# Two accumulators for the dense sums, one bank for all placings, four to five build banks, and blanks written by GpSimd

## The reference

```python
xn = _layernorm(x)                            # x: 6250 x 256, f32
h = segment_sum((xn @ W1)[src] * edge_weight[:, None], dst, 6250)
g = segment_sum((h @ W2)[src] * edge_weight[:, None], dst, 6250)   # 200000 edges, dst sorted
x = x + g + linear_attention(xn)              # 4 heads of 64: (q (LN(k)^T LN(v))) wo + bo
x = x + moe_top2(_layernorm(x))               # 16 experts, 256 -> 512 -> 256, then a layernorm
```

## Time and profile before

| | |
|---|---|
| median of 3 runs | 3532.04 us (3525.42 to 3533.8) |
| the profiled execution | 3563.73 us |
| its span | 3561.7 us |
| its mean granted TensorE clock | 0.906 of 2.4 GHz |

### The profile page before, as it was taken

One profiled execution on the slowest core, in us unless ns is written; L12 is line 12 of the kernel. 1 busy time (PEld: TensorE's weight loads), 2 busy tenths in 40 slices (PEclk: granted clock), 3 DMA queues, 4 the chain that ended last, 5 costly groups with the idle time before them and its releaser, 6 DMA issues.

```text
span 3561.7 us, 48771 instructions
## 1 busy us (share of the span) xinstructions
PE 2840.4 (80%) x14412; PEld 2015.7 (57%) x14413; DVE 1395.8 (39%) x3855; ACT 1370.9 (38%) x2993; POOL 1922.7 (54%) x2019
## 2 busy tenths in 40 slices
PE   1799999999999999788778787888877648999930
PEld 0466556566566656555555555555556647888820
DVE  8455545455554554322222222222225641111157
ACT  4687767777777773000000000000004423333322
POOL 2555555566565564466666666666643551222235
PEclk9999999999999999888888888989888868999975
DMA  6344344344444436655555555555532334444454
GB/s 217 118 154 155 115 151 156 117 160 157 145 131 155 155 120 199 197 161 161 160 158 167 161 163 158 164 156 164 162 106 84 116 123 132 139 145 133 125 156 122
DMA packets 268415, 527.04 MB, mean 148 GB/s; under 512 B 58823, under 2 KB 155086, under 8 KB 268096
## 3 DMA queue, kind: packets, MB, share of 16 engines
q0 software_dynamic: 88848, 240.99, 22.3%
q1 hardware_dynamic: 148256, 252.66, 21.7%
q10 hardware_dynamic: 31120, 31.04, 2.7%
HBM read 394.15 MB, written 131.79 MB: 148 GB/s over the span
## 4 chain that ended last, share of the span: by engine, by line
PE 54%; another core or an unknown queue 15%; issue 11%; DVE 7%; ACT 5%; DMA 4%; SPq 2%; ACTq 0%; DVEq 0%; POOL 0%; POOLq 0%
PE bank L994 23%; PE bank L982 12%; PE sums L1008 5%; PE bank L1217 4%; DMA pa<-ys_d 3%; PE bank L1205 2%; PE bank L1018 1%; PE bank L1078 1%; ACT build L795 1%; ACT build L793 1%; PE sums L965 1%; PE bank L1027 1%; PE bank L1144 1%; ACT pa L916 1%
## 5 line engine op out<-in xcount | busy, mean ns | idle before, releaser
L688 POOL DMA_INDIRECT pa<-xn_d,srcs x816 | 783.5, 960 | 537.7 <-PE sums L1008 321.5
L994 PE MATMUL bank<-t1s,pa 128*128 128x256 f32 x2450 | 643.4, 414 | 153.9 <-ACT ob L818 83.3
L688 POOL DMA_INDIRECT pa<-h_d,srcs x544 | 528.4, 971 | 307.2 <-issue 150.3
L994 PEld LDWEIGHTS bank<-t1s,pa 128*128 128x128 f32 x2450 | 497.3, 209 | 281.9 <-issue 121.5
L982 PE MATMUL bank<-build 128*128 128x343 f32 x1500 | 514.9, 484 | 138.8 <-DVE build L1376 60.9
L994 PE MATMUL bank<-t0s,pa 128*128 128x256 f32 x2450 | 558.7, 384 | 9.8 <-DVE pa L1394 8.0
L1394 DVE TENSOR_TENSOR pa<-bank,pa 128x343 f32 x750 | 378.0, 514 | 422.0 <-PE bank L982 183.7
L994 PEld LDWEIGHTS bank<-t0s,pa 128*128 128x128 f32 x2450 | 461.3, 191 | 108.6 <-issue 48.0
L982 PEld LDWEIGHTS bank<-build 128*128 128x128 f32 x1500 | 276.5, 197 | 350.0 <-issue 278.6
L795 ACT ACTIVATE build<-build,ones 128x343 f32<-128x343 f32 x750 | 436.3, 582 | 24.4
L793 ACT ACTIVATE build<-build,tabs 128x343 f32<-128x343 f32 x750 | 424.9, 567 | 41.1 <-issue 27.4
(11 more groups left out here) (257 smaller groups left out, 2716.2 us busy)
## 6 DMA issues: line engine op xcount, KB each, us to landing
slab_d<-pa SPq DMA_DIRECT2D x175, 448.0 KB
pa<-slab_d SPq DMA_DIRECT2D x175, 448.0 KB
pa<-in_w ACTq DMA_DIRECT2D x32, 512.0 KB, 3.9
pa<-in_w SPq DMA_DIRECT2D x32, 512.0 KB, 3.6
pa<-ys_d SPq DMA_DIRECT2D x109, 130.0 KB
pa<-xn_d,srcs POOLq DMA_INDIRECT x816
pa<-eo_d SPq DMA_DIRECT2D x49, 256.0 KB, 3.1
pa<-h_d,srcs POOLq DMA_INDIRECT x544
```

The source lines that it names most:

```text
L688: pool.indirect_dma_start(gath2[b * QT + j], None, table, bass.IndirectOffsetOnAxis(ap=srcs[:, n:n + 1], axis=0)).then_inc(s_g[b], 16)
L994: ins = pe.matmul(app[:, 0:D], slab3[:, s, :], table[:, s * D:(s + 1) * D], start=s == 0, stop=s == T - 1)
```

## The change

Bank 7, until now the dense placing's, becomes the second accumulator; the accumulators (banks 4 and 7) alternate by unit. Both kinds of placing share bank 6, so each waits for both kinds of add. Of the two accumulators the one that the present unit doesn't need is lent to the builds: from the start the bank whose turn isn't now the running sum's, and after the dense placing the other one too, so that a unit's first chunks have four banks and the later ones five. `wait` in `build_banks` is the number of adds of the unit that must be done before a chunk may be built. `free_for_dense` picks the place of the dense placing, in layer 0 the first chunk from 5 on, in layer 1 the first plane from 1 on, that has no step with a placing or an add of a group near it: chunk 5 in 16 units, 12 in 4, 19 in 4; plane 1 in 12 units, 2, 3 and 4 in 4 each. DVE's dense add follows at four chunks or one plane behind. GpSimd writes the blanks with a memset, in its gather queue ahead of the gathers whose ring slot is freed at that plane or just behind it; in most units that is two blanks, one step's four gathers, two blanks, four gathers, one, four, two, and then the other gathers.

```diff
-        bld, app, plg, pld = [bank[2], bank[3], bank[5]], bank[4], bank[6], bank[7]
+        app, plc = [bank[4], bank[7]], bank[6]
...
+        blanks_at = {}
+        for i in range(NU - 1):
+            for p in range(CT):
+                behind = min(s for n in range(p, CT) for s in steps_at(i, "p", n, 0))
+                blanks_at.setdefault(behind + RING, []).append((i, p))
...
+        def build_banks(i):
+            banks, last, use, wait = [2, 3, 5, (4, 7)[i % 2]], {}, [], []
+            for m in range(KB):
+                if i > 0 and m == dense_at[0][i] + 1:
+                    banks.append((7, 4)[i % 2])
+                b = min(banks, key=lambda b: last.get(b, -1))
+                use.append(b)
+                wait.append(last.get(b, -1) + 1)
+                last[b] = m
+            return use, wait
...
+            def blank_plane(i, p):
+                pool.wait_ge(s_ap, i * CT + p + 1)
+                pool.wait_ge(s_slab[p], i * 16 + 16)
+                pool.memset(plane(p), 0.0).then_inc(s_z, 1)
+
             for s in range(STEPS):
+                for i, p in blanks_at.get(s, ()):
+                    blank_plane(i, p)
                 gathers(s, 0, xn_d)
...
-                act.activation(ob[1][:], app[:, 0:D], ACT.Copy).then_inc(s_obd, 1)
+                act.activation(ob[1][:], app[i % 2][:, 0:D], ACT.Copy).then_inc(s_obd, 1)
...
-                pe.wait_ge(s_bev, c + 1)
-                pe.matmul(bld[c % BLD][:, 0:WT], lohot[c % LR], mvs[c % MR], start=True, stop=True
+                wait_from(pe, s_bev, i * KB + wait[m])
+                pe.matmul(bank[use[m]][:, 0:WT], lohot[c % LR], mvs[c % MR], start=True, stop=True
...
-                if p == 0 and d > 0:
-                    pe.wait_ge(s_obd, d)
+                if p == 0:
+                    wait_from(pe, s_obd, d - 1 if i > 0 else d)
...
                 pe.wait_ge(s_hpd, 2 * d + 2)
-                wait_from(pe, s_pad, d)
+                wait_from(pe, s_pag, placed[0])
+                wait_from(pe, s_pad, placed[1])
...
-                    if m == 2 and i > 0:
+                    if m == dense_at[0][i]:
                         place_dense(i - 1, 0)
...
-                    if p == 1 and i > 0:
+                    if p == dense_at[1][i]:
                         place_dense(i - 1, 1)
...
+                    if i > 0 and m == dense_at[0][i] + 4:
+                        place_add(1, GU + i - 1, t1s)
                     add_chunk(i, m, at)
...
+                    if i > 0 and p == dense_at[1][i] + 1:
+                        place_add(1, GU + i - 1, t0s)
                     all_gathered(steps_at(i, "p", p, 1), 1, t0s)
```

More of the change, by code:

```diff
@@ L431, in ring_of, with free_for_dense @@
             return s % size, used + s // size, size
+        def free_for_dense(i, layer, where, last, behind):
+            for at in range(last[0], last[1]):
+                so_far = STEPS * i // NU if not layer else STEPS * max(i - 1, 0) // (NU - 1)
+                near = []
+                for n in range(KB if where == "m" else CT):
+                    for s in steps_at(i, where, n, layer):
+                        if n < at:
+                            so_far = s + 1
+                        if at - behind <= n < at + behind:
+                            near.append(s % QK)
+                if (so_far - 1) % QK != 1 and 1 not in near and 2 not in near:
+                    return at
+            assert False
+        dense_at = [[None] + [free_for_dense(i, layer, "mp"[layer], ((5, 24), (1, 6))[layer], (4, 1)[layer])
+                              for i in range(1, NU)] for layer in range(2)]
+        def build_banks(i):
[8 more added lines that the diff above has]
+            return use, wait
+        build_at = [build_banks(i) for i in range(NU)]
         def chunk_at(m):
@@ L795, in moving @@
                 act.activation(a, a, ACT.Relu, bias=ones[:, 0:1], scale=-1.0).then_inc(s_mv, 1)
-            def blanks(i, p):
-                act.wait_ge(s_ap, i * CT + p + 1)
-                act.wait_ge(s_slab[p], i * 16 + 16)
-                act.activation(plane(p), zero[:].broadcast_to([P, CT * P]), ACT.Copy).then_inc(s_z, 1)
             def takes(steps, layer):
@@ L832, in _ @@
                             moving(i + 1, m)
-                        blanks(i, p)
                     takes(steps_at(i, "p", p, 0), 0)
@@ L1010, in gathered @@
                 ins.then_inc(s_hu, 1)
+            placed = [0, 0]
             def place_gathered(u, layer):
@@ L1391, in add_chunk @@
                 dve.wait_ge(s_bmm, c + 1 + CREDIT)
-                dve.wait_ge(s_bev, c + BLD - (0 if i == NU - 1 else 1))
+                wait_from(dve, s_bev, c if i == NU - 1 else c - 1)
                 part = slab3[:, :, bass.ds(at[chunk_at(m)], W)]
-                dve.tensor_tensor(part, bld[c % BLD][:, 0:WT].rearrange("p (s w) -> p s w", w=W), part, ALU.add
+                dve.tensor_tensor(part, bank[build_at[i][0][m]][:, 0:WT].rearrange("p (s w) -> p s w", w=W), part, ALU.add
                                   ).then_inc(s_bev, 1)
@@ L1494, in _ @@
                 for p in range(CT):
-                    if p == 0 and i > 0:
-                        place_add(1, GU + i - 1, t1s)
                     if (i, p) in halves_at:
```

27 lines of the change are left out of this document (14 added, 13 removed).

## The result

The changed kernel is **slower by 0.5%**: 3552.01 us (median of 6 runs, 3543.76 to 3567.85) against 3534.14 us (6 runs, 3525.42 to 3536.34), ratio 1.0052, 95% interval 1.0032 to 1.0072. Forecast were 3441 us and a range of 3370 to 3545.

The account below looks back on a forecast made before the run. PE's work was taken to bound layer 0, the loop between gathers and PE to pace layer 1. Terms -66 - 32 - 9 + 15 = -92 us took 3563.73 to 3471.7, scaled by 0.9911 to 3441 us; range 3370 to 3545.

Parts of the forecast that it names:

- Bound of layer 0: Layer 0: PE's own work bounds it, busy 1202.6 of 1282 us, so at most 79.4 us of idle PE can be had.
- Layer 1, -66: Layer 1, second accumulator: removing apply's wait for the copy was to save 66 us, bounds -10 and -150.
- the second limit: Layer 1, gather stream: GpSimd still pauses once per ring refill, 34 x 2.3 = 78 us stay, 83 of 161.5 go.
- The first limit, 75: Layer 1, apply's wait for the accumulator copy: 75 of 83.3 us go, about 8 come back at place_dense.
- Rival A: Layer 1: late PE completions only move to place_dense and ring slots; layer 1 gives -10, total 3496 us; chance 0.20.
- Layer 0, banks, -32: Layer 0, chunk builds: four and five banks remove PE's idle time before chunks, gaining 13.5 to 50.6 us, middle -32.
- the 1.45 us tail: Layer 0, later chunks of a unit: 1.45 us each instead of 0.58, read as PE and DVE waiting on each other.
- Accumulators, shared bank, later placing in layer 0, -9: Layer 0, dense placing moved from chunk 2 to 5 to 19: its wait for the copy goes, -9 us, between -6 and -14.
- Blanks on GpSimd, +15: Layer 0, unit starts: blanks in the gather queue cost +0.4 to +0.6 us a unit over 24 units, +15 us.
- The floor of layer 0, 1221 us: Layer 0, GpSimd's minimum: 979 us of gathers, 134 of blanks and 108 of ring refills, allowing up to -61 us.
- rival C: Layer 0: blanks lengthen the gather stream instead of filling pauses, GpSimd becomes the bound; slower, 3573 us; chance 0.14.
- Rival D: Layer 0, unit starts: GpSimd's memsets hold DVE through shared ports, at worst +38 us on the sum, 3478 us; chance 0.04.

## Why the prediction was wrong, point by point

**Bound of layer 0: right in name.** PE's work bounds it, and on the 3247 us chips without a gap. The 79.4 us of idle PE in the first trace were not missing banks: with three banks and half of the gathers PE is idle for 4 of 1050 us on the 3560 us chip.

**Layer 1, -66: wrong, measured -8 in the first traces and +2 on the 3560 us chip.** The step that failed is the second limit, that GpSimd would pause once in each refill, 34 times, and 83 of its 161.5 us would go. It rested on nothing but the size of the ring. GpSimd still waited 165.0 us. The first limit, 75, was no limit on time either: the 83.3 us wait for the copy did go from PE's list, but PE's idle time fell by 31 us and the layer by 8. Rival A, at -10 in this layer, had the size and half of the mechanism: what was late was PE's completion, as ACT and GpSimd together saw at 1829 us. It stayed at the slots of the ring, where GpSimd waited as before, and did not come back at the dense placing, where PE waited 2.2 us. The prediction named the lateness as its weak point and still gave A only 0.20. The lateness goes with the number of gathers, which halving them shows; why, and why only on some chips, is open.

**Layer 0, banks, -32: wrong in sign, +36 on the 3560 us chip.** The failed step is the reading of the 1.45 us tail as the round trip of three banks. A bank more would then have brought the pace back to that of free banks; with five it was still 1.45. (That pace is 0.61 us a chunk and not the 0.58 of the prediction: ten records in 3.05 us are five chunks. It changes nothing in the sum.) The other half of the error is the end of the unit: the applies wait for the last add, so chunks that end earlier bring nothing unless the adds do. In the first traces PE's last chunk ends 1.4 us earlier after the last apply (25.6 against 27.0 us) and the last add at the same time (27.8 both). What is gained is one longer wait, 36.5 us in place of 8.0, and the clock falls in it.

**Accumulators, shared bank, later placing in layer 0, -9: wrong, -50 on the 3560 us chip and +27 on the 3247 us chips.** The -9 priced the removed wait. On the 3247 us chips the new place of DVE's add is the likely cause, which was costed at nothing with "its mean wait for PE is 1.1 us" as cover. An average was taken for cover where a queue had none: 24 x 0.7 = 17 us was named as the price without it, and 27 came. Which of the three edits gives 50 us on the 3560 us chip isn't settled. What changed there can be read from one trace each. This is the window of layer 0 with all three and no more, to be held against the first of the earlier trace rows:

```profile
133.00:1363.00 1230.00, 1170.15 (x5657) 779.67 (x5656) 668.91 (x1758) 911.06 (x1640) 752.76 (x785) 0.99 0.46 152
```

Of the 52 us, 32 are shorter busy time of PE (1202.58 before) and 20 less idle time. The first part goes with the clock: within layer 0 it stood at its lower level for 82 us before and for 20 us with the three edits. The forecast priced the removed wait alone and had nothing in layer 0 for what the clock gives back.

**Blanks on GpSimd, +15: right in sign and mechanism, too small.** +28 us on the 3560 us chip (3580.29 - 3552.50) and +42 on the 3247 us chips. The step that was short is the pause: the four gathers ahead of the last pair were taken to swallow 2.2 us of pause, but on the 3247 us chips there is none at that place. Nor did the fourth bank make up for the late blank: with the whole change PE still waits 25.6 us for adds in front of chunks there, and not at all with ScalarE's blanks. Both costs are within the bounds of -17 to +75.

**The floor of layer 0, 1221 us, and rival C.** GpSimd's waits fell from 311.0 to 69.0 + 44.3 us, and the blanks waited 49.8 + 10.1 + 3.9 more; the blanks did fit the pauses. C's sign is the result's, its mechanism isn't: the queue is not the bound.

**Rival D, the ports.** The one-hots' mean went from 362 to 463 ns, 40 us more of DVE's time. This is as the row of the long memset said. The Trainium skill, page "SBUF — State Buffer", section "SBUF: two separate sides", has the rule that a two-port operation of VectorE and an operation of GpSimd keep each other out of a shared pair of ports for a whole instruction. Every trace here agrees: the mean is 361 to 367 ns in the kernels in which ScalarE blanks and 463 to 472 ns in those in which GpSimd does. What share of this lies on the path no run tells apart; on the 3247 us chips the later first adds alone account for 44 us where 42 are to be explained, which leaves little for it.

**The parts cancel.** On the 3560 us chip: -50 + 36 + 28 = +14 us. That the result is near zero says nothing of the parts; and no version was better on both kinds of chip: three banks with ScalarE's blanks is 0.9864 on the one and 1.0080 on the other. The change with ScalarE's blanks, 0.9967 and 1.0000, was slower on neither.

## What to carry to other kernels

When several engines hear of one engine's work late and all at once, a buffer behind that work may only move the wait: find what delays the completions (here by halving the gathers) before pricing the wait that shows it. Before adding banks to a producer, ask which consumer's last step closes the stage; if that doesn't come earlier, the producer only collects its idle time into one piece, where its clock may fall. Work that moves to an engine's queue costs by what stands ahead of it there, not by its length, and two jobs behind one wait cost the second's length too.

## What the runs showed of the hardware that was not expected

- The same kernel takes 3246 to 3248 us on three chips, 3550 to 3567 us on a fourth, and took 3534 us where it was first timed. The rows land as fast on both kinds, as far as the traces have the events: the last of a step lands 1.8 us in the median after its last gather has ended, in layer 0. On the slower kind PE's completions are late, by over 13 us at worst after the recorded ends, and adds can follow chunks at 1.45 us, while the granted clock in the records is 0.99.
- This lateness goes with the number of indirect gathers and not with their bytes: layer 0 takes 1334 us with all, 1332 with all at half the row size, and 1183 with half of them.
- After an idle PE of 4.14 us the granted clock was 0.55 for the next 6 us and a plane of applies took 6.0 us, not 3.3. The recorded waits ahead of such a fall needn't be as long: in layer 0 of the kernel before, the clock went to its lower level 14 times, 82 us in all, and only one of PE's recorded waits shortly before was longer than 2.1 us.
- A GpSimd memset of 128 x 896 f32 took 0.86 us, ScalarE's blank of the same size 0.94.
